# Opening loads moved into the first layer's own program, and two sets of attention stacks filled one memset at a time

## The reference

```python
x = x + _L0_attn_ref(_layernorm(x), wq, wk_down, wv_down, wk_up, wv_up, wo)   # L0a
x = x + _L0_xattn_ref(_layernorm(x), ctx_1024, w_q, w_k, w_v, w_o)            # L0x
x = x + _L0_ffn_ref(_layernorm(x), gate_w, w1, w2)                            # L0f
...
x = x + _L3_attn_ref(_layernorm(x), Wa, Wout_w, Wout_b)                       # L3a
x = x + _L3_xattn_ref(_layernorm(x), ctx_1024, ctx_1024, mask, Wq, ...)       # L3x
x = x + _L3_ffn_ref(_layernorm(x), router_w, ...)                             # L3f
```

## Time and profile before

| | |
|---|---|
| three runs, median (lowest, highest) | 2648.43 us (2644.59, 2655.07) |
| the profiled execution, its own time | 2639.58 us |
| its span, first to last instruction | 2637.8 us |
| mean granted TensorE clock over the span | 0.941 |
| busy PE, DVE, ACT, POOL | 2256.8, 1563.1, 1306.0, 716.2 us |

### The profile page before, as it was taken

The page is one execution under the profiler, slowest core; times in us unless marked ns, Lnnn a source line. Parts: engine busy times, 40 slices in busy tenths (PEclk is TensorE's granted clock), DMA queues, the critical chain, the costliest instruction groups (busy, mean ns, idle before and its releaser), DMA issues. The chain is left out here.

```text
span 2637.8 us, 48181 instructions
## 1 busy us (share of the span) xinstructions
PE 2256.8 (86%) x16479; PEld 1468.8 (56%) x16479; DVE 1563.1 (59%) x4614; ACT 1306.0 (50%) x3591; POOL 716.2 (27%) x982
## 2 busy tenths in 40 slices
PE   6969998878898489975769999887779998799989
PEld 4635544745555245543647766566647776466653
DVE  4757773146666588755266664553466776777730
ACT  3726662235555256652346766422235655366642
POOL 2123212544432432200733231234421111322100
PEclk9979998989999699996889999988989999899999
DMA  2033325120000133321700000265400000433200
GB/s 76 2 81 91 98 64 181 43 81 19 31 33 17 38 100 101 94 75 35 140 25 1 1 1 1 96 135 148 135 23 2 1 2 17 105 85 85 59 19 16
DMA packets 126657, 155.77 MB, mean 59 GB/s; under 512 B 22592, under 2 KB 89289, under 8 KB 125266
## 3 DMA queue, kind: packets, MB, share of 16 engines
q1 hardware_dynamic: 113858, 141.30, 18.9%
q0 software_dynamic: 8640, 8.31, 1.6%
q10 hardware_dynamic: 3920, 3.09, 0.6%
HBM read 117.83 MB, written 35.51 MB: 58 GB/s over the span
## 5 line engine op out<-in xcount | busy, mean ns | idle before, releaser
L584 ACT ACTIVATE L3x_p_ring<-L3x_ps_t 128x512 f32<-128x512 f32 x256 | 141.6, 598 | 104.0 <-PE L3x_ps_t L663 102.9
L467 DVE CUSTOM_DVE_ANT_0 L3x_ps_s<-L3x_ps_s,L3x_mask_q 128x512 f32<-128x512 f32 x256 | 170.0, 718 | 33.8 <-PE L3x_ps_s L642 32.4
L584 ACT ACTIVATE L1x_p_ring<-L1x_ps_t 128x512 f32<-128x512 f32 x256 | 137.7, 623 | 76.3 <-PE L1x_ps_t L661 76.1
L584 ACT ACTIVATE L0x_p_ring<-L0x_ps_t 128x512 f32<-128x512 f32 x256 | 137.8, 625 | 73.5 <-PE L0x_ps_t L661 73.5
L470 DVE TENSOR_REDUCE L0x_mx<-L0x_ps_s 128x2 f32<-128x1024 f32 x128 | 151.9, 1221 | 34.7 <-PE L0x_ps_s L642 34.3
L470 DVE TENSOR_REDUCE L1x_mx<-L1x_ps_s 128x2 f32<-128x1024 f32 x128 | 151.9, 1221 | 28.5 <-PE L1x_ps_s L642 27.2
L1006 ACT ACTIVATE L2a_probs<-L2a_ps_s,L2a_top 128x256 f32<-128x256 f32 x256 | 117.8, 472 | 78.5 <-DVE L2a_top L956 78.5
L661 PE MATMUL L3x_ps_t<-L3x_q_stack,L3x_k_stack 128*128 128x256 bf16 x512 | 120.2, 274 | 4.5 <-DMA L3x_q_stack<-L3x_m_rows 4.2
L1006 ACT ACTIVATE L3a_probs<-L3a_ps_s,L3a_top 128x128 f32<-128x128 f32 (+1 forms) x256 | 104.0, 422 | 38.4 <-DVE L3a_top L952 36.2
L663 PE MATMUL L3x_ps_t<-L3x_mask_k,const_ident_bf 128*128 128x256 bf16 x512 | 119.9, 274 | 0.0
L890 POOL COPY L3a_wide<-L3a_inverse 128x128 f32<-128x128 f32 x128 | 33.8, 293 | 226.8 <-DVE L3a_inverse L969 226.8
(11 more groups left out here) (711 smaller groups left out, 6019.3 us busy)
## 6 DMA issues: line engine op xcount, KB each, us to landing
L2f_w_e<-L2f_in_w_e SPq DMA_DIRECT2D x23, 544.0 KB, 3.7
L0x_k_stack<-L0x_k_dram SPq DMA_DIRECT2D x96, 96.0 KB
L1x_k_stack<-L1x_k_dram SPq DMA_DIRECT2D x96, 96.0 KB
L3x_k_stack<-L3x_k_dram SPq DMA_DIRECT2D x96, 96.0 KB
L0f_w<-L0f_in_w SPq DMA_DIRECT2D x32, 256.0 KB, 6.7
L1a_rk_wide<-L1a_rk_dram SPq DMA_DIRECT2D x8, 1024.0 KB, 4.7
L1f_w<-L1f_in_w SPq DMA_DIRECT2D x32, 256.0 KB, 3.5
kept_x<-ctxT SPq DMA_DIRECT2D x24, 256.0 KB, 3.4
```

Of the source, the lines that this page charges most:

```text
L467: last = dve.tensor_tensor_reduce(span, span, mask_q[:, t, :], 1.0, 2 * MASKED, ALU.add, ALU.max, accum_out=mx[:, t, k:k + 1])
L584: act.activation(p_ring[:, u % RING, j * BANK:(j + 1) * BANK], t_bank(o), ACT.Exp, scale=scale).then_inc(out["t"].sem, 1)
```

## The change

- The program `load_constants` is gone. `Opening.load` runs on SP in L0a's own program: the tiles of batch 0 of x (128 KB), `ident`, `minus_half`, then the six weights of L0a, then the other fourteen tiles of x, `causal_min`, the remaining 14 constants, and after them the weights of L0x.
- DVE waits for the first rows and the two constants ahead of ln(0), and for the other rows ahead of ln(1). PE waits for the weights as before.
- "absorb" moves in `order` from the front to unit -4, between ln_rest(0) and the unit of x(0) and ln(1). PE's own sequence is not changed by it, since ln and ln_rest are not PE's. On DVE it now stands behind ln(0) and ln_rest(0). DVE copies `causal_min` to bf16 there, ahead of its copy of `w_o`.
- The other six bf16 constants are copied by POOL at the entry "x" of batch 5 of L0a.
- The four memsets of a set of stacks are separated: one at each entry "x" of batches 1 to 4 (k of parity 1, k of parity 0, q of parity 1, q of parity 0). The stacks of L0x are filled inside L0a in this way, those of L3x inside L3a.

```diff
--- before.py
+++ after.py
@@ -64,13 +64,6 @@
 def cross_stacks(nc, ctx, name):
 
     return {n: ctx.enter_context(nc.sbuf_tensor(name + n + "_stack", [P, 2, 16, c], BF16)) for n, c in (("q", S), ("k", KX))}
-
-
-def fill_stacks(pool, stacks, filled):
-
-    for n, word in (("k", ONE_PAIR), ("q", 0.0)):
-        for par in range(2):
-            pool.memset(stacks[n][:, par].rearrange("p h k -> p (h k)").bitcast(F32), word).then_inc(filled, 1)
 
 
 class Semaphores:
@@ -697,7 +690,7 @@
         sem.clear()
 
 
-def attention_rows(nc, x_sb, const, w, cfg, ahead, follow, stacks):
+def attention_rows(nc, x_sb, const, w, cfg, ahead, follow, stacks, opening):
 
 
 
@@ -725,12 +718,12 @@
         if 0 <= b < B:
             order.append((kind, b, k))
 
-    if latent:
-        order.append(("absorb", 0, 0))
     for u in range(-2 * U, B * U + 2 * U + 1):
         b, part = divmod(u, U)
         first, second = cfg["slots"][part]
         ends = lambda i: i % GROUPS == GROUPS - 1
+        if latent and u == -U:
+            order.append(("absorb", 0, 0))
         put("scores", b, part)
         put("max", b, part)
         for kind, k, off in first:
@@ -854,7 +847,9 @@
 
             @block.sync
             def _(sp):
-                if ahead.own:
+                if opening is not None:
+                    opening.load(sp, x_sb, ahead)
+                elif ahead.own:
                     ahead.load(sp)
                 if not latent:
                     sp.dma_start(w_o[:], w["w_o"]).then_inc(w_o_in, 16)
@@ -871,8 +866,12 @@
 
                         pool.wait_ge(ln_done, b * LN_STEPS + 2 * QT + 1)
                         pool.tensor_tensor(rstd[:], mean_var[:, :, 1], const["minus_half"][:, 0:QT], ALU.pow).then_inc(ln_pool, 1)
-                    if kind == "x" and b == 2 and stacks is not None:
-                        fill_stacks(pool, stacks, filled)
+                    if kind == "x" and 1 <= b < 5 and stacks is not None:
+                        name_of, par = ("k", "q")[(b - 1) // 2], b % 2
+                        pool.memset(stacks[name_of][:, par].rearrange("p h k -> p (h k)").bitcast(F32),
+                                    ONE_PAIR if name_of == "k" else 0.0).then_inc(filled, 1)
+                    if kind == "x" and b == 5 and opening is not None:
+                        opening.round_others(pool)
                     if kind == "x" and out_bias:
 
                         pool.wait_ge(ln_done, (b + 1) * LN_STEPS)
@@ -905,10 +904,15 @@
                     g = b * C + k
                     if kind == "absorb":
 
+                        opening.round_causal(dve)
                         dve.wait_ge(absorbed, 2)
                         dve.tensor_copy(w_o[:].rearrange("p c k -> p (c k)"), ps_s[:, 1, 0:C * P]).then_inc(absorb_out, 1)
                     if kind == "ln":
 
+                        if opening is not None and b == 0:
+                            dve.wait_ge(opening.first_rows, 48)
+                        if opening is not None and b == 1:
+                            dve.wait_ge(opening.other_rows, 16)
                         for t in range(QT):
                             dve.bn_stats(stats[:, t, :], x_sb[:, b * QT + t, :]).then_inc(ln_done, 1)
                         dve.wait_ge(ln_done, b * LN_STEPS + QT)
@@ -3472,33 +3476,36 @@
         fidelity_tail(nc, x_sb, y_all, const, tail, name + "tail_")
 
 
-def load_constants(nc, const, x_sb, x, const_in, follow, stacks):
-
-    with ExitStack() as own:
-        sem = Semaphores(nc, own, "start_")
-        loaded, rounded, filled = sem("loaded"), sem("rounded"), sem("filled")
-        wide = {n: own.enter_context(nc.sbuf_tensor("wide_" + n, list(const_in[n].shape), F32)) for n in BF16_CONSTS}
-        with nc.Block() as block:
-
-            @block.sync
-            def _(sp):
-                sp.dma_start(x_sb[:], x.rearrange("b (t p) d -> p (b t) d", p=P)).then_inc(loaded, 16)
-                for n, a in const_in.items():
-                    sp.dma_start(wide[n][:] if n in wide else const[n][:], a).then_inc(loaded, 16)
-                if follow is not None:
-                    follow.load(sp)
-
-            @block.gpsimd
-            def _(pool):
-                fill_stacks(pool, stacks, filled)
-
-            @block.vector
-            def _(dve):
-
-                dve.wait_ge(loaded, 16 * (1 + len(const_in)))
-                for n in BF16_CONSTS:
-                    dve.tensor_copy(const[n][:], wide[n][:]).then_inc(rounded, 1)
-        sem.clear()
+class Opening:
+
+    def __init__(self, nc, ctx, wide, const, x, const_in):
+        names = ("first_rows", "other_rows", "causal_in", "others_in", "causal_ready", "others_ready")
+        (self.first_rows, self.other_rows, self.causal_in, self.others_in, self.causal_ready, self.others_ready) = (
+            ctx.enter_context(nc.semaphore("opening_" + n)) for n in names)
+        self.wide, self.const, self.const_in = wide, const, const_in
+        self.x = x.rearrange("b (t p) d -> p (b t) d", p=P)
+        self.others = [n for n in const_in if n not in ("ident", "minus_half", "causal_min")]
+
+    def load(self, sp, x_sb, weights):
+        sp.dma_start(x_sb[:, 0:QT, :], self.x[:, 0:QT, :]).then_inc(self.first_rows, 16)
+        for n in ("ident", "minus_half"):
+            sp.dma_start(self.const[n][:], self.const_in[n]).then_inc(self.first_rows, 16)
+        weights.load(sp)
+        sp.dma_start(x_sb[:, QT:NT, :], self.x[:, QT:NT, :]).then_inc(self.other_rows, 16)
+        sp.dma_start(self.wide["causal_min"][:], self.const_in["causal_min"]).then_inc(self.causal_in, 16)
+        for n in self.others:
+            sp.dma_start(self.wide[n][:] if n in self.wide else self.const[n][:], self.const_in[n]).then_inc(self.others_in, 16)
+
+    def round_causal(self, dve):
+        dve.wait_ge(self.causal_in, 16)
+        dve.tensor_copy(self.const["causal_min"][:], self.wide["causal_min"][:]).then_inc(self.causal_ready, 1)
+        dve.wait_ge(self.causal_ready, 1)
+
+    def round_others(self, pool):
+        pool.wait_ge(self.others_in, 16 * len(self.others))
+        for n in BF16_CONSTS:
+            if n != "causal_min":
+                pool.tensor_copy(self.const[n][:], self.wide[n][:]).then_inc(self.others_ready, 1)
 
 
 def decoder(nc, x, out, const_in, layers):
@@ -3529,7 +3536,8 @@
                  for n, a in const_in.items()}
         room, stacks = ExitStack(), {}
         stacks["L0x"] = cross_stacks(nc, room, "L0x_")
-        load_constants(nc, const, x_sb, x, const_in, follow.get("constants"), stacks["L0x"])
+        wide = {n: room.enter_context(nc.sbuf_tensor("wide_" + n, list(const_in[n].shape), F32)) for n in BF16_CONSTS}
+        opening = Opening(nc, ctx, wide, const, x, const_in)
 
         pool_dma = lambda n: ctx.enter_context(nc.semaphore(n))
         for name in ORDER:
@@ -3546,7 +3554,8 @@
                 if name == "L3a":
                     stacks["L3x"] = cross_stacks(nc, room, "L3x_")
                 attention_rows(nc, x_sb, const, layers[name], dict(ROWS[name], name=name + "_"), ahead[name], follow.get(name),
-                               stacks.get("L3x") if name == "L3a" else None)
+                               stacks["L3x"] if name == "L3a" else stacks["L0x"] if name == "L0a" else None,
+                               opening if name == "L0a" else None)
             else:
                 attention_cross(nc, x_sb, const, layers[name], dict(ATTENTIONS[name], name=name + "_"), ahead[name], stacks.get(name))
                 room.close()
```

## The result

| | before | after |
|---|---|---|
| median of 8 runs each | 2649.22 us | 2637.18 us |
| the profiled execution, its own time | 2639.58 us | 2637.29 us |
| its span | 2637.8 us | 2635.5 us |

The ratio is 0.9957, 95% interval 0.9943 to 0.9972: 11.4 us less, with 7.4 to 15.1 as its interval. The interval does not reach 1, but the change is smaller than the 0.5% that the prediction took as the line for telling it from none; it lies inside the forecast range. (One execution of each kernel, 4744 us before and 3351 us after, is disturbed and left out of the ratio.)

A forecast was written before the change was run, and what follows sets the result against it. PE, busy 86%, was taken as the bound, with touched places read from their timelines. Opening -11.2, L3a -2.3, L0a +0.3 sum to -13.2 us: 2635.2 from 2648.43; own range -10 to -16 (2632 to 2638), with other cases 2625 to 2645.

The forecast's parts named there:

- PE's start: Opening: PE's first matmul at 8.9 us instead of 17.81, ends 7.6 and 10.7, once `w_v` has landed.
- The order on DVE: Opening: layernorm runs beside absorb, so transposes come at 14.15 instead of 25.39; -11.2 us together with the earlier weights.
- The wait for `causal_min`: Opening, DVE ahead of the `w_o` copy: data in by 10.6, wanted at 13.6, so 3 us of cover.
- L3a: Four separate fills stall xn for 9.0 us in sum instead of 11.3: -2.3 us, ends 0 and -3.3.
- the clock's: L3a batch 2: TensorE's lower clock after PE's idle time costs up to 1.6 us; half, 0.8, was counted.
- L0a: New fills and six casts on POOL hold one two-element `tensor_scalar` by 0.85 us, partly absorbed: +0.3 us, ends 0 and +0.9.
- the first rival: Opening: TensorE's clock rises sooner, saving 5 us more; total -18.2, 2630 us; chance 0.17.
- the weights don't land first: Opening: later transfers share the DMA engines, PE starts at about 15; total -7.1, 2641.3 us; chance 0.13.
- four stalls cost as much as one: L3a: each stall lets TensorE's clock fall, the 2.3 us are gone; total -10.3, 2638.1 us; chance 0.10.
- every DVE operation is held: L0a and L3a: POOL's fills hold all DVE operations touching SBUF; slower, 2651 to 2659 us; chance 0.05.

The follow-up runs named there:

- the fills behind the bias: Kernel after, with each memset issued on POOL behind the addition of the output bias to x_sb: 2629.21 us beside 2647.63 of before, ratio 0.9935.
- before again: The kernel before, unchanged, profiled a second time: one execution, 2645.04 us, 319.1 us in L3a.
- the last version: Kernel after, fills behind the output-bias addition, absorb's four weights loaded first, other rows behind `causal_min`: 2622.16 us beside 2650.47 of before, ratio 0.9906.

## Why the prediction came out right

The forecast was 13.2 us less; the ratio says 11.4 (7.4 to 15.1). By its steps:

- **PE's start:** 8.9 forecast, 8.98 measured, with `w_v` as releaser. The agreement to a tenth is luck: 8.9 was chosen between 7.6 and 10.7, and with this order of loads seven executions started between 8.84 and 10.04, with the old order three between 17.81 and 18.69. What the working got right are the releaser and the two ends. The second issue took 0.45 us and `w_v` was issued at 4.59 (5.1 or 6.3 forecast): the 1.64 of the earlier trace rows did come from the 1 MB ahead of it. `w_v` then took 4.3 us to land, 4.4 before. The queue serves roughly in order: the other rows behind it did no harm that shows, ahead of it they cost 2.2 us.
- **The order on DVE:** transposes at 14.15 forecast, 14.24 measured, for the reason given; absorb first again loses 2.3 of it.
- **The wait for `causal_min`:** it cost nothing, but its cover was mis-sized. The cast begins at 12.81 and the copy of `w_o` at 13.76: 0.95 us of cover, of which the cast takes 0.29, and not 3. The forecast had `causal_min` in by 10.6, with issues at a pitch of 0.48 us; its own issue, behind the 896 KB of x, took 3.03, and it was there 2.1 us later than forecast.
- **L3a:** 9.0 of stalls forecast, 8.3 measured, against 11.3. The row lengths forecast for xn (3.8, 3.9, 2.2, 2.2) included the undisturbed 0.59 on top of the hold; measured are 3.29, 3.46, 1.75, 1.76, so each hold is about half a microsecond shorter than said. Batches 3 and 4 cost 0.7 each, not 1.1; batch 2 costs 3.9, not 3.6. The term that was mis-sized is the clock's: the forecast had 2.8 of waiting and half of 1.6 for the clock, measured are 2.4 of PE's idle time and so 1.5 for the rest. The granted clock is 0.65 over 1974 to 1978 us, at the lower level (0.50) from 1976 to 1978, and 1.00 at the same place with the fills behind the bias; behind the fills of q it is 1.00, as forecast. Gain 3.0 to 3.7 (stage with and without) instead of 2.3.
- **L0a:** +0.3 forecast. The one held row is there, 0.82 us:

```profile
40.07 3.52 POOL L871 MEMSET L0x_k_stack<- 128x4096 f32 x1
...
42.79 0.82 DVE L923 TENSOR_SCALAR L0a_mean_var<-L0a_mean_var 128x2 f32<-128x2 f32 x1
...
45.83 0.29 POOL L889 COPY L0a_wide<-L0a_inverse 128x128 f32<-128x128 f32 x1 [1.44 <-DVE L0a_inverse L973]
...
52.00 0.53 POOL L889 COPY L0a_wide<-L0a_inverse 128x128 f32<-128x128 f32 x2 [5.65 <-DVE L0a_inverse L973]
```

  The copies to `wide` around it stand at 39.60, 45.83 and 52.00, before at 49.88, 56.10 and 62.29: 10.28, 10.27 and 10.29 earlier. The hold cost nothing in PE's path; the slack of DVE took it. The whole block says the same: from the first transposes to L0x are 125.6, 126.0 and 126.4 us in the three executions with the old opening, and 125.9 to 126.3 in the five with the new one and these fills in which TensorE's clock rose at the usual place. The six casts on POOL took 3.3 us (3.4 forecast), from 79.92 to 83.22, and rstd followed at 83.93 behind DVE, not behind them: no hold.
- **TensorE's clock:** the first rival is refuted. The windows view gives 1.00 for the whole opening, so the first rise is not in it and is read from the length of a group of four matmuls. In L3a, where the view has both levels, such a group took 2.07 us at a granted clock of 0.50 (before, at 1941.38) and 1.13 us at 1.00 (after, at 2015.10). In the opening of the kernel after:

```profile
28.87 2.08 PE L1062 MATMUL L0a_ps_m<-L0a_xT,L0a_w_q 128*128 128x256 f32 x4
...
33.41 1.13 PE L1062 MATMUL L0a_ps_m<-L0a_xT,kept_a 128*128 128x256 f32 x4
```

  So the rise came between 17 and 19 us behind the transposes, before between 17 and 18. PE's idle time ahead of the transposes was 2.3 us shorter (0.62 against 2.94), and that did not bring the rise forward; in no run did it come sooner. It can come later, as in the second execution of after:

```profile
33.59 2.08 PE L1062 MATMUL L0a_ps_m<-L0a_xT,kept_a 128*128 128x256 f32 x4
```

  This, and a fall of the clock near L0a's end, spread the time to L0x. In that execution the last rstd of L0a comes 84.8 us behind the first transposes and L0x 43.5 behind it; in the first execution of after it is 83.4 and 42.5. The second part goes with the granted clock from 14 to 6 us ahead of L0x, 0.57 there and 0.79 in the first. With the memset in four pieces both are late too (the group at 33.74 takes 2.08). In these two executions L0x comes 128.3 and 128.5 us behind the first transposes, in the nine others without fills in a row at batch 2 of L0a 125.6 to 126.4.
- **Other rivals:** that the weights don't land first (PE at 15) is refuted by 8.98, that four stalls cost as much as one by 315.4 us with that edit alone, that every DVE operation is held by the copy that runs at 0.56 inside a memset, and by the whole time.

The stages that the change touches give 10.5 (the mean to L0x, 151.9 over three executions of the old opening, less 141.4 over the four with the opening and L0a as after) + 3.2 = 13.7. The 2.3 us between that and 11.4 are less than what one kernel differs from itself in the blocks between. But they have the same sign in every version with the new opening: by the stages (against the mean of before and before again in L3a) the whole gained 3.6 us too little with the opening alone, 5.9 with the fills behind the bias, 3.2 with absorb first and 2.8 in the last version. With the old opening and L3a's fills alone the stage gives 3.3 and the whole 3.2. This goes with the 1770.4 and 1776.9 us above. Each sum by stages lies inside the interval of the whole or at its upper edge (11.5 against 11.4 with the opening alone, 12.2 against 12.2 with absorb first), each rests on one profiled execution, and three of the five are held against the same runs of before. So that the new opening gives some 3 us back behind L0a is a sign and not shown; the prediction had no term for it, and its cause stays open. In part the total is so close because errors cancel: the two stages gained 13.7, a little more than forecast, the whole a little less.

## What to carry to other kernels

In this kernel a fill on POOL costs time only through the `tensor_scalar` of DVE that it overlaps, and through what waits for that one. Put it behind the instruction of POOL that waits for DVE's last `tensor_scalar` of a batch; spreading fills evenly is not enough. Here the same memsets in L3a cost 8.3 us or nothing, by the place of one `if`. Load first what the first matmul reads, and let the layernorm of the first rows run beside it. Judge changes of a few microseconds by their own stage: 3 us in L3a were plain there and lost in the whole time.

## What the runs showed of the hardware

- **The hold on DVE outlives the instruction.** The Trainium skill, SBUF — State Buffer, section "Who interferes with whom", has the pair locked for the whole instruction of the engine that came first. In the earlier trace rows, in the memset in pieces (3.41 of 3.63 us) and in L0a's fills in a row (7.77 us, from the middle of the first of four to the end of the fourth) the held `tensor_scalar` waited through all the memsets queued behind the first. So in these cases the trace disagrees with one instruction as the length of the hold. The opening alone shows the other case, where the trace agrees: a `tensor_scalar` that came just behind the start of the second memset was held from 4.29 to 7.72 and got in at the boundary between the second and third. What decides at a boundary was not found.
- **Which operations are held.** The same section's list names `copy`, `cast` and `tensor_scalar`, with suitable operands, as able to take the shared pair. The runs agree for `tensor_scalar` within SBUF, down to two elements (0.82, 3.43 and 7.77 us for one of 0.17). Maxima and copies from PSUM, statistics and a small reciprocal ran at their usual length beside memsets, unless they stood in DVE's queue behind a held one. No row looked at here has a `copy` or `cast` within SBUF beside a memset.
- **A large DMA can hold the queue's next issue**: 3.03 us behind 896 KB (2.67 to 3.94 over the seven executions with this order), against 0.43 to 0.47 usually. It depends on what stands ahead: with the same 896 KB fourth in the queue the next issues took 0.83, 0.43 and 0.64, and in the last version, where they are eleventh, the next took 1.52 and the third 1.30.
